# A graph layer's drain: half of the selector tiles made by GpSimd in place of VectorE

## The reference

```
msg_in = concat([x[src], x[dst], edge_attr])          # 100000 x 384
h   = msg_in @ W + b                                  # W is 384 x 128
h   = (h - mean(h)) * rsqrt(var(h) + 1e-5) * gamma + beta
out = segment_sum(relu(h), src, 6250)
return layernorm(x + out)
```

## Time and profile before

| what | us |
|---|---|
| median of 3 runs | 1759.11 (1758.96 to 1759.60) |
| the profiled execution, device time | 1758.61 |
| its span, first to last instruction | 1756.8 |
| PE busy | 1201.1 (68%) |
| DVE busy | 949.3 (54%) |
| ACT busy | 711.4 (40%) |
| POOL busy | 771.9 (44%) |

### The profile page before, as it was taken

One profiled execution on the slowest core, in us unless ns is written; L12 is line 12 of the kernel. 1 busy time (PEld: TensorE's weight loads), 2 busy tenths in 40 slices (PEclk: granted clock), 3 DMA queues, 4 the chain that ended last, 5 costly groups with the idle time before them and its releaser, 6 DMA issues.

```text
span 1756.8 us, 36181 instructions
## 1 busy us (share of the span) xinstructions
PE 1201.1 (68%) x9913; PEld 1049.7 (60%) x9914; DVE 949.3 (54%) x2787; ACT 711.4 (40%) x2814; POOL 771.9 (44%) x810
## 2 busy tenths in 40 slices
PE   6598776666766666766666666667666667656775
PEld 5455666655666556666566666566555656655662
DVE  7623355545555445554455555455455455538997
ACT  3223343433434333443334333344344344335766
POOL 0335544455444455444554444554445554450003
PEclk9767777878878788787888778788888777878998
DMA  7665455344443444444444443444444444312322
GB/s 213 170 129 137 127 154 147 111 127 131 129 115 116 124 131 129 120 115 125 126 130 130 115 128 113 131 130 127 112 120 126 131 128 128 111 54 80 92 65 73
DMA packets 192458, 215.22 MB, mean 123 GB/s; under 512 B 51350, under 2 KB 141802, under 8 KB 192272
## 3 DMA queue, kind: packets, MB, share of 16 engines
q1 hardware_dynamic: 166236, 160.39, 35.1%
q0 software_dynamic: 25088, 51.83, 8.5%
q10 hardware_dynamic: 948, 0.79, 0.2%
HBM read 144.85 MB, written 68.06 MB: 121 GB/s over the span
## 4 chain that ended last, share of the span: by engine, by line
PE 39%; another core or an unknown queue 24%; issue 18%; ACT 10%; DVE 6%; DMA 2%; DVEq 1%; SPq 0%; ACTq 0%
PE bank L962 11%; PE bank L940 7%; PE bank L916 7%; ACT late L1183 5%; PE bank L856 5%; PE bank L930 3%; PE bank L969 2%; ACT turn L1145 1%; DVE late L1580 1%; PE bank L846 1%; DMA tabB<-room 1%; PE bank L844 1%; ACT late L1189 1%; DVEq L493 1%
## 5 line engine op out<-in xcount | busy, mean ns | idle before, releaser
L683 POOL DMA_INDIRECT rows<-p,pos_idx x784 | 756.0, 964 | 825.3 <-ACT p L1149 535.0
L1145 ACT COPY turn<-bank 128x512 f32<-128x512 f32 x196 | 115.0, 587 | 688.0 <-remote 523.3
L962 PE MATMUL bank<-wc,turn 128*128 128x128 f32 x1552 | 297.2, 351 | 66.9 <-ACT turn L1145 59.9
L940 PE MATMUL bank<-room 128*128 x2592 | 246.4, 250 | 106.6 <-issue 61.4
L962 PEld LDWEIGHTS bank<-wc,turn 128*128 128x128 f32 x1552 | 257.4, 251 | 88.1 <-ACT turn L1145 79.3
L940 PEld LDWEIGHTS bank<-room 128*128 128x128 bf16 x2592 | 204.3, 115 | 128.0 <-issue 117.6
L1183 ACT ACTIVATE late<-room 128x128 f32<-128x128 f32 x864 | 256.4, 303 | 2.7 <-issue 1.3
L916 PE MATMUL bank<-late 128*128 128x129 f32 x1472 | 230.3, 299 | 33.9 <-issue 31.4
L1580 DVE SCALAR_TENSOR_TENSOR late<-room,late,floor 128x128 f32<-128x128 f32 x864 | 248.1, 349 | 0.4 <-issue 0.3
L916 PEld LDWEIGHTS bank<-late 128*128 128x128 f32 x1472 | 207.5, 214 | 26.4 <-issue 26.0
L1175 ACT COPY room<-bank 128x512 bf16<-128x512 bf16 x216 | 127.0, 588 | 223.9 <-remote 128.8
(11 more groups left out here) (240 smaller groups left out, 1256.1 us busy)
## 6 DMA issues: line engine op xcount, KB each, us to landing
p<-in_edge_attr_dram SPq DMA_DIRECT2D x98, 512.0 KB
room<-rows SPq DMA_DIRECT2D x256, 129.0 KB
near_bc<-near SPq DMA_DIRECT2D x98, 256.0 KB
late<-rows SPq DMA_DIRECT2D x176, 129.0 KB
rows<-p,pos_idx POOLq DMA_INDIRECT x784
win<-tabB SPq DMA_DIRECT2D x196, 31.5 KB
rows<-fill SPq DMA_DIRECT2D x24, 193.5 KB
tabB<-room SPq DMA_DIRECT2D x12, 384.0 KB, 3.8
```

The lines of the kernel that those rows point to most:

```text
L683: nc.gpsimd.indirect_dma_start(rows_ap, bass.IndirectOffsetOnAxis(pos_idx[:, k, j:j + 1], 0), stage[:, k, j, :], None).then_inc(st_free[k] ...
L940: mm = pe.matmul(bank[A_BANK + b2][:, jj * D:(jj + 1) * D], selT[b2][:, jj * P:(jj + 1) * P], tabA[:, bass.ds(at[jj // UJ], 1), part, :], ...
L962: pe.matmul(bank[H_BANK + h][:, t * D:(t + 1) * D], eT[h][:, t * P:(t + 1) * P], wc[:, 2, :], start=(t == 0), stop=False, skip_group_check ...
L1145: nc.scalar.copy(eT[h], bank[E_BANK][:]).then_inc(eT_ready, 1)
```

## The change

In the drain, from pair 180 on, VectorE's `selectors` makes the tiles of the first unit alone (one instruction of 128x256). GpSimd makes the two tiles of the second unit, with one `tensor_scalar` each (128x128, `iota_row` compared with the node number as a scalar of each partition), after its scatters. It waits for the same load and the same `n_o` as VectorE, and reports by a new semaphore, `n_selg`. TensorE waits for that too before it turns the selectors.

```
+        n_selg = sem("pool_selectors_made")
...
+        SHARED = FUSED + 6
+
+        def shared(s, lag):
+            return not below(s, lag, SHARED)
...
+            def later_selectors(s, c, q, r):
+                kk, hk, free = sel_at(s, c, 2, False), hs_at(s, c, q, r, 2), sel_free(s, 2, False)
+                pool.wait_ge(hs_ready[hk[0]], hk[1] * 32)
+                pool.wait_ge(n_o, free)
+                settle()
+                for j in range(UJ, SJ):
+                    a = nc.gpsimd.tensor_scalar(sel[kk][:, j, :], iota_row[:], hs[hk[0]][:, j, D:ROW], None, ALU.is_equal)
+                a.then_inc(n_selg, 1)
+
+            def step(s, c, q, r, on):
+                if on(2) and shared(s, 2):
+                    later_selectors(s, c, q, r)
+            drain_trips(pool, trip_count(pool), step)
+
             pool.wait_ge(n_run, (trip_count(pool) * PAIRS + LOOPED) * 2)
...
-            def turn_selectors(s, c, fused=False):
+            def turn_selectors(s, c, fused=False, drained=False):
                 pe.wait_ge(n_sel, s + 2)
+                if drained and shared(s, 1):
+                    pe.wait_ge(n_selg, s + (2 - SHARED))
...
-                    turn_selectors(s, c)
+                    turn_selectors(s, c, drained=True)
...
-            def selectors(s, c, q, r, numbers, fused=False):
+            def selectors(s, c, q, r, numbers, fused=False, drained=False):
...
-                nc.vector.tensor_tensor(sel[kk], numbers.unsqueeze(1).to_broadcast([P, SJ, P]),
-                                        hs[hk[0]][:, :, D].unsqueeze(2).to_broadcast([P, SJ, P]), ALU.is_equal).then_inc(n_sel, 1)
+                n = UJ if drained and shared(s, 2) else SJ
+                nc.vector.tensor_tensor(sel[kk][:, 0:n, :], numbers.unsqueeze(1).to_broadcast([P, n, P]),
+                                        hs[hk[0]][:, 0:n, D].unsqueeze(2).to_broadcast([P, n, P]), ALU.is_equal).then_inc(n_sel, 1)
...
-                    selectors(s, c, q, r, iota_row[:])
+                    selectors(s, c, q, r, iota_row[:], drained=True)
```

## The result

The changed kernel takes 1766.61 us, the kernel before 1757.47 us (medians of 7 runs each). The ratio is 1.0058, with a 95% interval of 1.0038 to 1.0078: slower, as forecast, by 9.1 us where the forecast had 4.7. The predicted 1764 lies 2.6 us from the measured median. But the profile shows that the loss came another way than the forecast said, so that the number is near by luck.

A forecast was written before the change was run, and what follows sets the result against it. VectorE was taken to bound the drain at 2.88 us a step. Collisions of 0.40 us less 0.27 saved gave +0.13 us x 36 = +4.7 us on 1758.61, with 0.5 for the median 1764 us; range 1750.5 to 1772.

The forecast's parts named there:

- The bound before, VectorE at 2.88 us: Drain: VectorE's six pieces of work in a row set the pace, 2.88 us a step.
- 2.38 us of TensorE: Drain step: TensorE from its transposes to its last product, giving 2.60 us a step, level with VectorE's shortened 2.61.
- some 0.6 us over two steps: Drain: slack said to hide the transposes' later start at a loop trip's start, 0.52 us after `add_pair`, not 0.14.
- Saved on VectorE, 0.27 us: Drain: VectorE's selector instruction falls from 512 to 256 columns, saving 0.27 us a step, 9.7 us over 36 steps.
- GpSimd's instruction, 0.28 us: Drain: each 128x128 `tensor_scalar` on GpSimd takes 0.28 us, two of them 0.56 us a step.
- The upper bound, 0.36 us from a two-input product: Drain: most that GpSimd's 128-column `tensor_scalar` would take, from a two-input product at 2.05 ns a column.
- The new wait on TensorE, costed at nothing: Drain: TensorE's wait for `n_selg` lengthens a step only if GpSimd's lateness exceeds the slack over two steps.
- two collisions that push VectorE by 0.40 us: Drain: GpSimd's SBUF reads block VectorE's two-input work, 0.20 us per instruction, 0.40 us a step against 0.27 saved.
- a sign of being wrong: Profile after: forecast wrong if messages keep their 1.14 us, or GpSimd's instructions are much shorter than 0.2 us.
- rival 3: Drain: GpSimd bounds if its `tensor_scalar` takes 0.6 us or more; 3.5 us a step, up to 1781 us; chance 0.06.
- Its ring of parts: Drain, rival 3: 1.34 us to `sum_pair`'s end, up to 0.9 start, 1.2 work, 0.06: 3.5 us a step.
- rival 2: Drain: GpSimd waits for VectorE, transposes come some 0.5 us later; -1 to +4 us, 1758 to 1763; chance 0.22.

The follow-up runs named there:

- the run with half the selectors: Kernel before, with the selectors of a pair's second unit left out from pair 180 on, made by no engine: ratio 1.0005 to before, step 2.86 us.
- the late load: Kernel before without the second unit's selectors, TensorE loading its two block numbers after the sum, not at the step's start: ratio 0.9940, step 2.68 us.
- unit first, late load: Changed kernel, TensorE summing a pair's second unit first and loading block numbers after the sum: ratio 0.9992 to the kernel before, step 2.87 us.
- a lighter or a shorter ring: Changed kernel with one GpSimd tile (1.0034 to before), one two-input GpSimd instruction (1.0038), or TensorE summing the second unit first (1.0013).

## Why the prediction was right in sign and mostly wrong in mechanism

- **The bound before, VectorE at 2.88 us:** right. What was missed is how close the next one lay. The step in question is "2.38 us of TensorE", from which the prediction made 2.60 us a step. It counted from the transposes to the last product and left out what lies between there and the next transposes. In the run with half the selectors the same work takes 2.19 us (the select is 1.03 us there and not 1.20) and the rest 0.57; together TensorE needs 2.76 us, and 2.86 in the mean of a trip. The gain had a ceiling of 0.02 us a step, not 0.18 to 0.27. The run with half the selectors shows it, and the late load shows that the rest is the register load. The slack of "some 0.6 us over two steps" was misread too: in the earlier trace rows the select ends at 1614.29 and the `add_pair` that needs it starts at 1614.65, so with 0.06 us of hand-over it was 0.3.
- **Saved on VectorE, 0.27 us:** right. The selectors fell from 0.68 us to 0.42, and with the load moved the step is 2.61.
- **GpSimd's instruction, 0.28 us:** mis-sized by more than half. It is 0.60 us alone and 0.75 in place, and the sum took the price of the collision from it. The upper bound, 0.36 us from a two-input product, was no bound: `tensor_scalar` is the slower kind here, with one input.
- **The new wait on TensorE, costed at nothing:** 0.09 us a step where TensorE's stream is the bound.
- **The deciding term, two collisions that push VectorE by 0.40 us:** it didn't happen in the changed kernel, where messages kept 346 ns and the four of them 1.13 us, which the prediction itself had named as a sign of being wrong. GpSimd starts 0.9 to 1.2 us into the messages, at their end, and is itself the one that waits. Where it starts 0.1 to 0.2 us into them (unit first, late load), VectorE is pushed, by 0.23 us for both instructions together, not 0.40; a single two-input instruction 0.6 us into them pushed it by 0.36.
- **What was true instead** is rival 3, GpSimd as the bound, which had a chance of 0.06. Its ring of parts was right (1.34 us to the end of the sum, start, work, 0.06); with the measured 0.19 us of start and 1.38 to 1.59 of work it gives 2.98 to 3.26 us for the plain steps; with the start of a trip, where TensorE's branch and load end last, the mean is 3.16. Half of rival 2 was true with it: GpSimd's work grows by 0.3 us a pair because its first instruction waits for VectorE.

From the runs the step adds up so: 2.88 before, down to TensorE's 2.86, up by 0.09 for the second wait to 2.95, and the other 0.21 are the ring, of which a lighter or a shorter ring gives back 0.18 to 0.20. The predicted number came near by luck: 0.40 us of push that wasn't there less a saving of 0.27 that wasn't there either is +0.13, with the sign of the true +0.26 and half its size.

What stays open is whether a fifth buffer for GpSimd's tiles, which would open the ring, would pay: no run has it. By the runs above TensorE's 2.95 us would then be the bound, unless the load is moved too.

## What to carry to other kernels

Before taking work from the engine that bounds a loop, work out each other engine's whole period, from one start of an instruction to its next start and not from its first to its last instruction: the part between can hold register loads and waits that the busy times don't show, and the label "waited for X" covers them when X happens to end late. Look at the distance between the end of X and the start: 0.05 us was a real wait here, 0.34 and 0.51 us were not. Leaving the work out altogether is the cheapest test of what moving it can bring. When work moves to an engine that must wait for a buffer and be waited for, write down the ring that it closes and put the measured duration of that very kind of instruction in it.

## What the runs showed of the hardware

- GpSimd's one-input `tensor_scalar` (0.60 us for 128x128, 0.91 for 256 columns, 1.23 for 384) is slower than its two-input `tensor_tensor` (0.39 and 0.61). A scalar from memory costs 0.08 us more than a constant (0.60 against 0.52).
- The pairing of GpSimd and VectorE in SBUF reads is real, but who pays depends on when GpSimd starts and on its kind of instruction. Two `tensor_scalar` from the start of a row of four two-input VectorE instructions on pushed VectorE by 0.23 us. From the middle of the row on VectorE lost 0.04 us or nothing by them, and GpSimd's instructions grew from 0.60 to 0.94 us (two a step) or 1.22 us (one a step). A two-input `tensor_tensor` of 128x256 in the middle of the row took 0.73 us and pushed VectorE by 0.36. The Trainium skill (SBUF — State Buffer, Who interferes with whom) calls the shared pair of ports an exclusive lock, and says of VectorE's two-port modes that the loser blocks for the whole instruction; here VectorE was held for 0.23 us by a pair of instructions of 1.27 to 1.38 us, and for 0.36 by one of 0.73, both times less than the instructions last, so for such a dense row the measurement decides against the letter of it.
- A wait on a long fulfilled semaphore costs TensorE 0.09 us, a load of two numbers into its registers half a microsecond (its record is 0.54 us long), and the branch at the start of a loop trip some 0.4 us more (3.14 against 2.76 us), when they stand in front of its first matmul of a step. Behind the sum the load cost nothing that could be seen.
